# Moving the first parts of A between the halves of kT, and the first half of Wq ahead of x

## The reference, cut to what matters

```python
x = x + tanh(g_xattn) * attn(layernorm(x), ctx)         # ctx (2, 64, 256), 16 heads of 64
x = x + tanh(g_ffn)   * moe(layernorm(x))               # 8 experts, F = 1024, top 2 per batch
# attn: softmax((h @ Wq) . (ctx @ Wk * 64**-0.5)) . (ctx @ Wv) @ Wo + bo     Wq, Wk, Wv (256, 1024)
# moe: router on the mean over a batch's tokens; out = sum of w_e * (gelu(h @ w1[e] + b1[e]) @ w2[e] + b2[e])
```

## Time and profile before

| what | value |
|---|---|
| median of 3 runs | 323.33 us |
| profiled execution, its own time | 322.94 us |
| span of that execution, first to last instruction | 320.8 us |
| PE busy, DVE busy, ACT busy, POOL busy | 314.4, 233.7, 164.1, 78.8 us |
| granted TensorE clock | 1.000 |
| DMA moved | 17.35 MB, nearly all of x and of the attention weights in the first 23 us |

### The profile page before, as it was taken

The page is one execution under the profiler, slowest core; times in us unless marked ns, Lnnn a source line. Parts: engine busy times, 40 slices in busy tenths (PEclk is TensorE's granted clock), DMA queues, the critical chain, the costliest instruction groups (busy, mean ns, idle before and its releaser), DMA issues.

```text
span 320.8 us, 5745 instructions
## 1 busy us (share of the span) xinstructions
PE 314.4 (98%) x1881; PEld 272.1 (85%) x1881; DVE 233.7 (73%) x563; ACT 164.1 (51%) x577; POOL 78.8 (25%) x158
## 2 busy tenths in 40 slices
PE   7899999999999999999999999999999999999996
PEld 7887988988999999988788888888887899888896
DVE  1889997978889999999998475466667554442643
ACT  2548555686766668775466254444533442321320
POOL 1325448484455536335600000000000000000000
PEclk9999999999999999999999999999999999999999
DMA  6992000000000017600007250000020000000011
GB/s 224 395 197 4 2 3 0 0 3 3 0 0 3 0 52 246 230 1 0 2 0 263 55 208 1 0 0 0 8 102 24 2 0 2 0 0 0 2 65 65
DMA packets 20765, 17.35 MB, mean 54 GB/s; under 512 B 11068, under 2 KB 16900, under 8 KB 20612
## 3 DMA queue, kind: packets, MB, share of 16 engines
q1 hardware_dynamic: 20464, 16.51, 17.0%
q10 hardware_dynamic: 276, 0.52, 0.5%
HBM read 14.93 MB, written 2.10 MB: 53 GB/s over the span
## 4 chain that ended last, share of the span: by engine, by line
PE 88%; DVE 7%; DMA 2%; issue 1%; ACT 1%; SPq 0%; DVEq 0%
PE ps L1098 26%; PE ps L1100 26%; PE ps L1099 26%; PE ps L1183 4%; DMA xt<-in_x_dram 2%; PE ps L1272 1%; PE ps L1118 1%; DVE mx L850 1%; PE ps L1156 1%; DVE pT_lo L808 1%; PE ps L1214 1%; PE ps L1370 1%; ACT sx L580 1%; DVE stats L729 1%; DVE sm L819 1%
## 5 line engine op out<-in xcount | busy, mean ns | idle before, releaser
L667 ACT ACTIVATE gel<-ps,b1sel 128x512 f32<-128x512 f32 x64 | 43.9, 690 | 95.5 <-PE ps L1100 95.4
L1057 DVE CAST h_hi<-gel 128x512 fp32r<-128x512 f32 x64 | 28.4, 443 | 58.7 <-ACT gel L667 58.5
L580 ACT ACTIVATE sx<-ps,mx 128x64 f32<-128x64 f32 x128 | 38.3, 327 | 27.6 <-DVE mx L850 27.6
L1098 PE MATMUL ps<-yT_hi,w_hi 128*128 128x512 f32 (+1 forms) x128 | 50.5, 395 | 0.0
L1099 PE MATMUL ps<-yT_lo,w_hi 128*128 128x512 f32 (+1 forms) x128 | 50.0, 390 | 0.0
L1100 PE MATMUL ps<-yT_hi,w_lo 128*128 128x512 f32 (+1 forms) x128 | 49.9, 390 | 0.0
L1059 DVE TENSOR_TENSOR h_lo<-gel,h_hi 128x512 fp32r<-128x512 f32 x64 | 44.9, 702 | 2.2
L466 POOL TENSOR_TENSOR sx<-sx,rs 128x512 f32<-128x512 f32 x32 | 33.2, 1058 | 48.0 <-DVE rs L824 47.8
L1098 PE MATMUL ps<-h_hi,w_hi 128*128 128x512 f32 x96 | 38.4, 400 | 0.0
L1100 PE MATMUL ps<-h_hi,w_lo 128*128 128x512 f32 x96 | 37.5, 390 | 0.0
L1099 PE MATMUL ps<-h_lo,w_hi 128*128 128x512 f32 x96 | 37.4, 390 | 0.0
(11 more groups left out here) (145 smaller groups left out, 672.7 us busy)
## 6 DMA issues: line engine op xcount, KB each, us to landing
stage_w<-in_L_ffn_w_dram SPq DMA_DIRECT2D x7, 1024.0 KB, 7.3
out_dram<-xt SPq DMA_DIRECT2D x6, 256.0 KB, 2.5
wqT<-in_L_xattn_Wq_dram SPq DMA_DIRECT2D x2, 512.0 KB, 7.9
wv_sb<-in_L_xattn_Wv_dram SPq DMA_DIRECT2D x2, 512.0 KB, 9.3
wo_sb<-in_L_xattn_Wo_dram SPq DMA_DIRECT2D x1, 1024.0 KB, 13.7
xt<-in_x_dram SPq DMA_DIRECT2D x1, 1024.0 KB, 10.7
stage_w<-in_L_ffn_w_dram SPq DMA_DIRECT2D x2, 512.0 KB, 4.4
wk_sb<-in_L_xattn_Wk_dram ACTq DMA_DIRECT2D x1, 512.0 KB, 4.2
```

The costliest lines, as they stand in the source:

```text
L580: last = nc.scalar.activation(sx[:, par, c0:c0 + M], ps[:, 2 * par + 1, c0 - BANK:c0 - BANK + M], ACT.Exp, bias=mx[:, par, h:h + 1], accum ...
L667: nc.scalar.activation(gel[:, f % 4, :], ps[:, h_bank, :], ACT.Gelu, bias=b1sel[:, b, slot, f:f + 1]).then_inc(gelu_done, 1)
L1057: nc.vector.tensor_copy(h_hi[:, f % 4, :], gel[:, f % 4, :]).then_inc(hhi_ready, 1)
L1098: mm(acc, hi_w, hi_x, start=start, stop=False)
```

## The change

Six edits. (1) `x`, Wk, Wv and Wq are laid out in DRAM so that each load reads one contiguous block; what lands in SBUF is the same, and each partition's run keeps its length (2 KB for Wk, Wv halves and for two tiles of x, 4 KB for Wq halves). (2) SP issues Wq's first half second, ahead of x tiles 0-1, and Wq's second half ahead of x tiles 2-3. (3) PE runs score pairs 0 and 2 between kT 0 and kT 1, after the tiny matmul. (4) The order of `groups`, the banks and ACT's order follow. (5) `x_norm(0)` covers tiles 0 and 1 alone; tiles 2 and 3 become a part of their own, with DVE's 8 instructions after x_low(1) and the Newton rounds on POOL in step -1, ahead of xn of tile 2. (6) The stats of tiles 2 and 3 move behind a_lo of part 3.

```diff
-        setup_groups = [("ctxT", 0), ("kT", 0), ("kT", 1)]
-        groups = setup_groups + A0 + V0 + late_groups
+        groups = [("ctxT", 0), ("kT", 0)] + A0[:4] + [("kT", 1)] + A0[4:] + V0 + late_groups
...
-        GRP_BANK = dict(zip(groups, [0, 1, 2, 3, 4, 5, 6, 0, 1, 3, 4, 2, 6, 4, 5, 0, 6] + [0, 1] * len(LATE)))
+        GRP_BANK = dict(zip(groups, [0, 1, 0, 2, 3, 4, 1, 5, 6, 1, 2, 3, 6, 4, 5, 0, 6] + [0, 1] * len(LATE)))
...
-        X_PARTS = [(0, TB // 2), (TB // 2, TB), (TB, NT)]
-        X_BY_DVE = X_PARTS[1][0]
+        X_PARTS = [(0, 2), (2, TB // 2), (TB // 2, TB), (TB, NT)]
+        X_BY_DVE = X_PARTS[2][0]
...
             sp.dma_start(ctx_sb[:, :], ctx_tokens.rearrange("b m d -> (b m) d")).then_inc(ld_ctx, 16)
+            sp.dma_start(wqT[:, 0:NP // 2, :], Wq[0]).then_inc(ld_wq[0], 16)
             load_x(0, 0, 0, 2)
-            sp.dma_start(wk_sb[:, :, HD // 2:HD], Wk.rearrange("(k p) n -> p k n", p=P)[:, :, HD // 2:HD]).then_inc(ld_wk[1], 16)
+            sp.dma_start(wk_sb[:, :, HD // 2:HD], Wk[1].rearrange("k p n -> p k n")).then_inc(ld_wk[1], 16)
+            sp.dma_start(wqT[:, NP // 2:NP, :], Wq[1]).then_inc(ld_wq[1], 16)
             load_x(1, 0, 2, TB // 2)
-            for half in range(2):
-                blocks = slice(half * NP // 2, (half + 1) * NP // 2)
-                sp.dma_start(wqT[:, blocks, :], Wq[:, blocks, :]).then_inc(ld_wq[half], 16)
...
+                if s == -1:
+                    newton(*X_PARTS[1], rstd1, ve_x, 2)
                 if s == 1:
-                    newton(*X_PARTS[1], rstd1, ve_x, 2)
+                    newton(*X_PARTS[2], rstd1, ve_x, 3)
...
             group("kT", 0)
+            for g in A0[:4]:
+                group(*g)
             group("kT", 1)
-            for g in A0[:7]:
+            for g in A0[4:7]:
                 group(*g)
...
             x_stats(0, range(0, 2))
-            x_stats(1, range(2, TB // 2))
             x_norm(0)
...
-            for g in A0[:6]:
+            for g in A0[:4]:
+                group(*g)
+            x_stats(1, range(2, TB // 2))
+            for g in A0[4:6]:
                 group(*g)
             x_low(0)
             for g in A0[6:]:
                 group(*g)
             x_low(1)
+            x_norm(1)
             x_stats(2, range(TB // 2, TB))
...
             group("kT", 0)
-            group("kT", 1)
             pe.wait_ge(rows_ready, 1)
             pe.wait_ge(tanh_done, 1)
             mm(ps[:, 7, 0:2], ones_row[:, :], tg_row[:, :], start=True, stop=True).then_inc(tg_spread, 1)
-            for i in range(0, 8, 2):
-                score_pair(i)
+            score_pair(0)
+            score_pair(2)
+            group("kT", 1)
+            score_pair(4)
+            score_pair(6)
...
+_X_BLOCKS = [(0, 0, 2), (0, 2, 4), (0, 4, 8), (1, 0, 8)]
...
+    if name == "x":
+        b, s, d = a.shape
+        a = a.reshape(b, 128, s // 128, d)
+        a = _np.concatenate([a[i, :, t0:t1, :].reshape(-1) for i, t0, t1 in _X_BLOCKS])
     if name == "L0_xattn_Wq":
-        a = a.T.reshape(-1, 128, a.shape[0]).transpose(1, 0, 2)
+        a = a.T.reshape(2, -1, 128, a.shape[0]).transpose(0, 2, 1, 3)
+    if name in ("L0_xattn_Wk", "L0_xattn_Wv"):
+        a = a.reshape(a.shape[0] // 128, 128, 2, -1).transpose(2, 0, 1, 3)
```

More of the change, by code:

```diff
@@ L17, in gated_cross_attention_moe_kernel @@
     P = 128
-    B, S, D = x.shape
-    M = ctx_tokens.shape[1]
-    HD = Wv.shape[1]
+    B, M, D = ctx_tokens.shape
+    S = out.shape[0] // B
+    HD = 2 * Wv.shape[-1]
     DH = 64
@@ L38, in gated_cross_attention_moe_kernel, with x_block @@
     assert 2 * DH == P and 2 * M == P and B * M == P and TOP == 2 and NCH == 2 and KD == 2
-    x_rows = x.rearrange("b (p t) d -> p b t d", t=TB)
+    def x_block(b, t0, t1):
+        first = next(n for n, (part, u0, u1) in enumerate(_X_BLOCKS) if part == b and u0 <= t0 and t1 <= u1)
+        assert _X_BLOCKS[first] == (b, t0, t1)
+        start = sum(P * (u1 - u0) * D for _, u0, u1 in _X_BLOCKS[:first])
+        return x[start:start + P * (t1 - t0) * D].rearrange("(p t d) -> p t d", p=P, d=D)
     out_rows = out.rearrange("(b p t) d -> p b t d", b=B, t=TB)
@@ L350, in load_x @@
             def load_x(i, b, t0, t1):
-                sp.dma_start(xt[:, b * TB + t0:b * TB + t1, :], x_rows[:, b, t0:t1, :]).then_inc(ld_x[i], 16)
+                sp.dma_start(xt[:, b * TB + t0:b * TB + t1, :], x_block(b, t0, t1)).then_inc(ld_x[i], 16)
             sp.dma_start(ctx_sb[:, :], ctx_tokens.rearrange("b m d -> (b m) d")).then_inc(ld_ctx, 16)
+            sp.dma_start(wqT[:, 0:NP // 2, :], Wq[0]).then_inc(ld_wq[0], 16)
             load_x(0, 0, 0, 2)
-            sp.dma_start(wk_sb[:, :, HD // 2:HD], Wk.rearrange("(k p) n -> p k n", p=P)[:, :, HD // 2:HD]).then_inc(ld_wk[1], 16)
+            sp.dma_start(wk_sb[:, :, HD // 2:HD], Wk[1].rearrange("k p n -> p k n")).then_inc(ld_wk[1], 16)
+            sp.dma_start(wqT[:, NP // 2:NP, :], Wq[1]).then_inc(ld_wq[1], 16)
             load_x(1, 0, 2, TB // 2)
             for half in range(2):
-                blocks = slice(half * NP // 2, (half + 1) * NP // 2)
-                sp.dma_start(wqT[:, blocks, :], Wq[:, blocks, :]).then_inc(ld_wq[half], 16)
-            for half in range(2):
                 cols = slice(half * HD // 2, (half + 1) * HD // 2)
-                sp.dma_start(wv_sb[:, :, cols], Wv.rearrange("(k p) n -> p k n", p=P)[:, :, cols]).then_inc(ld_wv[half], 16)
+                sp.dma_start(wv_sb[:, :, cols], Wv[half].rearrange("k p n -> p k n")).then_inc(ld_wv[half], 16)
             load_x(2, 0, TB // 2, TB)
@@ L467, in step @@
                                                 ALU.mult).then_inc(mul_done, 1)
+                if s == -1:
+                    newton(*X_PARTS[1], rstd1, ve_x, 2)
                 if s == 1:
-                    newton(*X_PARTS[1], rstd1, ve_x, 2)
+                    newton(*X_PARTS[2], rstd1, ve_x, 3)
                     pool.sem_inc(x_rstd, 1)
                 if s == 4:
-                    newton(*X_PARTS[2], rstd1, ve_x, 3)
+                    newton(*X_PARTS[3], rstd1, ve_x, 4)
             pool.wait_ge(guess_ready, 1)
@@ L489, in _ @@
         def _(act):
-            act.dma_start(wk_sb[:, :, 0:HD // 2], Wk.rearrange("(k p) n -> p k n", p=P)[:, :, 0:HD // 2]).then_inc(ld_wk[0], 16)
+            act.dma_start(wk_sb[:, :, 0:HD // 2], Wk[0].rearrange("k p n -> p k n")).then_inc(ld_wk[0], 16)
             act.dma_start(gg[:, 0:1], g_xattn.rearrange("(o n) -> o n", o=1)).then_inc(ld_g, 16)
@@ L797, in step @@
                 if s == 4:
-                    x_norm(2)
+                    x_norm(3)
                 if s in (6, 10):
@@ L865, in step @@
                     out_bias(0)
-                    x_norm(1)
+                    x_norm(2)
                 if s == 1:
```

## The result

The changed kernel takes 324.36 us, median of 6 runs (324.30 to 324.71), against 323.07 (322.87 to 323.44, 6 runs). The ratio is 1.0041 with a 95% interval of 1.0028 to 1.0053: slower by 1.3 us. The forecast was 322.83, which is 0.5 under the 323.33 of the first three runs, with a range of 322.1 to 323.9. The profiled execution took 324.30 us, with a span of 322.3 against 320.8 before.

The account below looks back on a forecast made before the run. TensorE bounds, busy 314.4 of 320.8 us, with DVE full early; idle time lies ahead of 14.2. Gain 18.0 - X = 0.54, rounded to 0.5, takes 322.94 to 322.44; the median's 0.39 makes 322.83, range 322.1 to 323.9.

Parts of the forecast that it names:

- X: Start of x_low(1) on DVE, 18.43 before: later of 17.47 (PE, ACT) and x's landing + 9.72; taken as 17.47.
- 2 x 0.90: Score pairs 0 and 2 on PE before kT 1: 16 matmuls cost 0.90 us, from 48 at 2.95 and 16 at 1.16.
- list of PE's waits: PE's early stretch: waits of 1.23 and 0.6 us go, two of 0.6 for ACT's copies come; PE gains 0.96.
- the rule on queues: Counter-rule: ACT's queue still moves Wk's first half at 3.9 to 5.0 us, now beside 4 KB pieces; kT 0 waits.
- the paragraph on VectorE: DVE's early work: tile 0's maxima start at X + 2.84, 20.31 instead of 20.50; gain behind `out_bias` 0.54 us.
- The sum: Whole kernel: gain 18.0 - X by DVE and by GpSimd, 0.54 us, staying to the end.
- The paragraph on GpSimd: Newton done at 22.7, xn of tiles 2 and 3 at 24.0 and 25.35; tile 0's product can start at 25.4.
- Loads: Early loads: x tiles 0-1 land at 7.3 to 8.3, taken 7.7; Wk's second half at 9.0 to 10.0, taken 9.3.
- The layouts "at zero": Removing strides in DRAM costs zero; bounded by the slow stretch going away, x tiles 0-1 about 1 us earlier.
- rival (a): Early loads get quicker: Wk's first half 0.4 earlier, x tiles 0-1 by 7.3; gain 0.9, 322.4; chance 0.35 with gains over 0.65.
- Rival (b): Newton on GpSimd becomes the bound from X = 18.0; loss 0.9, 324.2; chance 0.17 with all losses over 0.65.
- A sign that the prediction names for being wrong: PE's transposes of tile 2: xn of tile 2 is what PE waits for at 24 us, later than 24.3.

Follow-up runs that it names:

- e6: Kernel before with only the order of loads changed, old layouts, norm over four tiles as before; 326.01 us, ratio 1.0095.
- e7: Changed kernel with the old strided layouts of x, Wk, Wv and Wq; 324.69 us, ratio 1.0049.
- e3: Kernel before with 9 needless two-input subtractions on GpSimd between xn of tile 3 and the product of tile 0; 323.76 us, ratio 1.0023.
- e5: As e3 on the kernel before, but the 9 needless GpSimd instructions are tensor_scalar with one SBUF input; 324.40 us, ratio 1.0043.
- e8: Kernel before with contiguous layouts of x, Wq and Wv, Wk strided as before; 322.21 us, ratio 0.9977.
- e1: Changed kernel with x_norm(1) moved from behind x_low(1) to right behind the stats of tiles 2 and 3; 323.49 us, ratio 1.0016.
- e10: Kernel before with contiguous layouts and the norm of tiles 2 and 3 split off, both norms at the start; 323.72 us, ratio 1.0023.
- e11: e10 with one number changed, so GpSimd starts xn of tile 0 only after x_norm(1) is done; 322.51 us, ratio 0.9984.
- e2: Changed kernel with each norm's three tensor_scalar instructions written as scalar_tensor_tensor, two small memsets more at the start; 324.29 us, ratio 1.0056.
- e12: e1 with Wk's first half issued by SP, between ctx and Wq's first half, instead of by ScalarE; 323.30 us, ratio 1.0007.
- e9: e1 with Wk strided as before; 323.40 us, ratio 1.0009.

## Why the prediction was wrong

**Where the time goes, in the prediction's own terms.** It forecast 0.54 gained where the changed kernel lost 1.13, 1.67 apart: 0.59 from X, 1.18 from a term that was missing, less 0.10 in how far `out_bias` and the rest of DVE moved.

**X was 18.06, not 17.47.** ACT's copy of kT 0 started 0.35 later than before; the prediction had kT 0 "as before". ctx landed 3.3 us after its issue instead of 2.6, Wk's first half 4.6 instead of 4.2, and PE began kT 0 at 5.50 where the kernel before has:

```profile
5.15 1.95 PE L1118 MATMUL ps<-ctxT,wk_sb 128*128 128x128 f32 x16
```

The other 0.24 lies in the score pairs and hand-overs. From the start of pair 0 to that of kT 1 it took 1.99 (8.18 to 10.17), not 2 x 0.90 = 1.80. The difference of 48 and 16 matmuls gives the slope alone, and every run of pairs also has its own start, which the prediction dropped for pairs 0 and 2. Its own list of PE's waits could have warned: waits of 1.23 and 0.6 go and two of 0.6 come, which is 0.63 gained and not 0.96. Measured are 0.42 ahead of pair 0 and 0.69 ahead of pair 4, so 0.72, less the 0.35 of kT 0: the 0.37 by which X came forward.

The lateness of kT 0 was weighed under the rule on queues and called unproven. Order alone (e6, e7) let Wk's first half land 4.5 and 4.4 us after its issue, against 4.2, 4.2 and 4.3 where the loads are those of the kernel before (before, e3, e5); e8, with the old order and Wk's old layout, had 4.9. So the 4 KB pieces of Wq ahead are not needed for the delay, and the runs don't show that the queues' turns are the cause. What is shown is the exposure: before, kT 0 could be 0.5 late at no cost (e3).

**The step that failed is the paragraph on VectorE.** With X as measured its formula holds: maxima at X + 2.84 = 20.90, measured 20.91, and a gain behind `out_bias` of 18.0 - 18.06 = -0.06, measured +0.04. The sum then carries `x_norm(2)` over at its old length, "Nothing behind it waits for a load or for anything else fixed in time". It took 2.37 instead of 1.19. e1 and the pair e10, e11 show that it is the meeting with GpSimd's xn instructions. e3 shows that adding such a meeting to the kernel before costs it 0.7 us. The paragraph on GpSimd had the times in hand: xn of tiles 2 and 3 from 22.7 to 25.35, and the kernel before runs that norm at 23.75 to 24.94, as shown above. It asked who waits for GpSimd and not what its instructions do to a neighbour.

The Trainium skill, GPSIMD Engine Reference, section 8. Key points, says that GpSimd shares its SBUF interfaces with VectorE and that there is "contention with DVE instructions in a 2-port perf mode or with two SBUF inputs". By that rule, the trace agrees for two inputs: tensor_tensor (0.53, 0.58 in e10) and scalar_tensor_tensor (0.46 to 0.58 in e2) were held, while a_lo, with one input in PSUM, kept its length beside xn, and so did bn_stats (0.76 for two in e10). The tensor_scalar instructions with one input were held as well (0.47 to 0.59); that fits only if they ran in such a mode, which no run shows. The prediction has nothing of this. Newton's instructions are 0.20 to 0.24 us long; the ones that did the holding are 0.61.

**Loads.** x tiles 0-1 at 7.3 were in the range of 7.3 to 8.3, and Wk's second half held nobody. The layouts "at zero" were wrong on their own: 0.8 us in the kernel before, much less in the changed one, whose chain no longer goes through x. Of rival (a) the half on x came true, 0.4 us earlier than with the old layouts (7.33 against 7.74 in e7), but Wk's first half came later and not earlier.

**Rival (b)** had the right side and the wrong mechanism. X stood at the point that it named, 18.0, so newton alone cost nothing. A sign that the prediction names for being wrong did come: PE's weight load for the transposes of tile 2 waited for xn until 24.67, later than 24.3. It cost nothing, since the scores behind them were done before DVE, which was late by the norm, took them up without a gap at 29.19. The product of tile 0 waited 1.22 us for DVE's reciprocal, not for GpSimd:

```profile
27.11 2.04 POOL L471 TENSOR_TENSOR sx<-sx,rs 128x512 f32<-128x512 f32 x2 [1.22 <-DVE rs L836]
```

**Left open.** The copy of kT 0 is later in nearly all variants for two reasons that the traces tell apart, and neither has a shown cause. One is the landing of Wk's first half: 4.2 or 4.3 us after its issue with the loads of the kernel before, 4.4 and 4.5 with the new order alone, 4.6 to 5.0 with any of the new layouts (e12 aside, where SP issues it), e8 and e9 included, where Wk keeps its own. The other is PE: in e3, e6, e7 and e12 the 16 matmuls of kT 0 took 2.11 to 2.60 us instead of 1.95 to 2.05, and the six fillers ahead 1.49 instead of 1.12, at a granted clock of 1.00. e3 has them with the loads of the kernel before, so they are no effect of the change.

ctx lands 3.3 to 3.7 us after its issue where Wk's contiguous first half is issued beside it on ScalarE's queue and 2.1 to 2.9 elsewhere, e12 included, where it stands behind ctx on one queue; why is not known. Each is one execution.

## What to carry to other kernels

An instruction has a price for its neighbours too. When work moves in time on GpSimd, lay its new interval beside DVE's and look for DVE's tensor_tensor, scalar_tensor_tensor and tensor_scalar instructions that read SBUF only; give each that can meet a GpSimd instruction the length of that instruction as its bound. Letting GpSimd wait until DVE's short chain is through can be faster than starting it early.

Before taking a wait off a chain, ask what the next chain starts from and how steady that is. And measure the parts of a bundle alone: here the layouts alone were worth 0.8 us in the kernel before, and the changed kernel is 2.1 behind that version. A small block of work moved out of one meeting can also delay the next engine in a new place, as `x_norm(1)` ahead of x_low(0) did in e1.

## What the runs showed of the hardware

A GpSimd instruction held DVE's at the grain of one instruction: a DVE instruction of 0.15 to 0.17 us on 128x4 elements that began while a GpSimd tensor_tensor of 0.61 us was running ended 0.01 to 0.04 behind it, after 0.46 to 0.59. The size of DVE's operand did not matter (128x2 in e10, 128x4 elsewhere), nor did one input or two among the three kinds named above. GpSimd's xn instructions took 0.61 to 0.63 beside them, as elsewhere 0.61.

What decides is which began first. In the changed kernel L717 began at 23.94, L719 at 24.55 and L721 at 25.25, each 0.02 to 0.06 ahead of GpSimd's next at 24.00, 24.57 and 25.27, and each kept its 0.15 to 0.17. Those that began 0.06 to 0.18 behind one were held (L718 at 24.13, L720 at 24.63, L723 at 25.45). The traces of e2, e3 and e10 show the same. In e5, with one input on GpSimd, it was not so strict. The tensor_reduce and the reciprocal behind the norm, one SBUF input each, kept their 0.69 and 0.25 us there beside GpSimd.

A subtraction with two SBUF inputs on 128x256, the second one broadcast along the row, took GpSimd 0.61 us; a multiplication by a constant with one input took 0.85 in e5.

The profiled execution of e10 took 325.3 us against its median of 323.72, because the clock fell in it. The row has the busy us by engine, then the clock:

```profile
16.20:19.40 3.20, 3.20 (x18) 3.20 (x17) 2.45 (x5) 1.16 (x3) 1.83 (x5) 0.53 1.05 351
```

The granted clock was 0.53 of full, near the 1.2 GHz level of the two, and vT 0 took 3.43 us instead of 1.95. Ahead of it PE had stood idle for 1.70 us and then been busy for 1.4. A wait alone does not tell when it falls: in e6 PE stood idle for 1.62 us until 9.34 and the clock stayed at 1.00. The execution that is e10's median had a clock of 1.00, so this is no part of what e10 shows on the norm, which ended at 13.4.
